# Rows of the two expert mixtures moved by list from GpSimd, with the root of a tile ahead of its two transfers

## The chip, the cores and the metric

One core of one Trainium2 chip runs the whole kernel in one launch. The metric is the device time of an execution in microseconds (us), the median of several. Lower is better.

## What is computed

Eight sequences of 512 tokens with 256 features pass through eight blocks in a row, each added to the residual stream: cross attention, a mixture of experts with layer norms inside (m0), cross attention, a "quantum" feed-forward, windowed attention, a second mixture of experts (m2), cross attention, and a ternary feed-forward. The change is in the two mixtures and in what follows them. The first one is

```python
gates = softmax(xf @ gate_w); topw, topi = top_k(gates, 2)        # 8 experts, 2 for each token
topw = topw / topw.sum(-1, keepdims=True)
h = gelu(_ln(einsum('td,edh->teh', xf, w1) + b1, ln1_g, ln1_b))   # 512 hidden features
y = einsum('teh,ehd->ted', h, w2) + b2
out = _ln(einsum('ted,te->td', y, combine) + xf, ln_g, ln_b)
```

The second has 1024 hidden features, no norm inside and none at its end. Each token is worked on by its two experts alone, so its row of 256 numbers has to come to the tiles of these experts, and the two results have to come back to the token.

## The kernel before

4096 tokens stand in SBUF as 32 tiles of 128 (`NT`), four to a batch (`TPB`), eight batches (`NB`). 8192 (token, expert) pairs fill at most 71 tiles of 128 rows (`NTILES`), each owned by one expert. A mixture has three stages, each a block with one instruction stream per engine, and the next block begins when all engines have ended this one.

1. `dispatch`. Batch by batch VectorE normalises (L909), TensorE transposes (L856) and forms the logits (L864), ScalarE copies, VectorE picks the two experts and works out the place of each pair (`route`, `ROUTE_STEPS` small operations one after the other), TensorE sums the counts (L872, L873). GpSimd then scatters the 128 rows of each tile twice into the DRAM tensor `sorted_in`, one indirect DMA for each tile and choice (L1042, 64 in all), and 8 more for padding (L1047).
2. `experts` (m0) and `experts_gelu` (m2). SyncE loads the 71 tiles in order (L1146, L1329), ScalarE stores the results to `sorted_out` (L1205, L1392). There are two buffers for tiles on their way in (`xin`) and two for results (`y`). In m0 TensorE's order at step j is: the four transposes of the hidden tile j (L1175), layer 1 of tile j+2 (L1166), the two transposes of the input tile j+3 (`turn`, L1157), layer 2 of tile j (L1185). VectorE's order at step j is: `hidden(j+2)` (bias and statistics, L1235 to L1241), the result y(j) (L1255), `centre(j+2)` (L1245). GpSimd takes the root of a tile's variance (L1271), and for the first 32 tiles it also adds a bias to two tiles of the residual stream at every second tile (L1280). At the start of the stage SyncE also loads five constants and the next attention's weights.
3. `combine_norm` (m0): GpSimd gathers two rows for each token (L1496, 64 indirect DMAs, each with its own wait for a free buffer), ScalarE scales the first (L1525), GpSimd adds it (L1507), VectorE adds the second (L1534), takes the norm (L1546, L1550), adds it to the stream (L1553) and takes the statistics of the next norm. After m2 there is no such stage: the next attention (`Arrival`) gathers the rows itself on GpSimd (L290).

TensorE's wait for tile j at `turn` is a wait for that tile's load; a load of tile j may begin when tile j-2 has been transposed (`xT_ps`, L1145). Each engine runs its own instructions strictly in the order written.

Of the kernel before, what the change touches and what calls it, by code (L numbers as in the profile page):

```python
# [23 lines left out]
P = 128  # L24
# [15 lines left out]
CAP = (NT + 1) * P  # L40
# [13 lines left out]
C_REGION = C_J + NTILES  # L54
C_PART = C_REGION + E
C_N = C_PART + 1


def constants():
# [12 lines left out]
    c[:, C_REGION:C_REGION + E] = CAP * np.arange(E)  # L72
    c[:, C_PART] = p
    return c
# [33 lines left out]
class Core:  # L108


    def __init__(self, nc, ctx, a):
# [4 lines left out]
        self.zeroed, self.padded = sem("zeroed"), sem("padded")  # L116
        self.scattered = [sem(f"scattered{s}") for s in range(2)]
        self.g_in = [sem(f"g_in{r}") for r in range(RING)]
        self.y_in = [sem(f"y_in{r}") for r in range(2 * TPB)]
        self.mixtures, self.gathers = 0, 0  # L120
# [15 lines left out]
        self.xs = nc.dram_tensor("sorted_in", [E * CAP + P, D], F32, kind="Internal").ap()  # L136
        self.ys = nc.dram_tensor("sorted_out", [NTILES * P, D], F32, kind="Internal").ap()
        self.pos = [sb(f"pos{j}", [P, NT], U32) for j in range(TOPK)]
# [12 lines left out]
RING = 4  # L151
# [45 lines left out]
def load_stage(nc, k):  # L197
# [3 lines left out]
    with ctx:  # L201
        zero_set, ones_set = sem("ld_zero_set"), sem("ld_ones")
        with nc.Block() as block:
# [12 lines left out]
            def _(pool):  # L216
# [4 lines left out]
                pool.dma_start(k.xs[E * CAP:E * CAP + P, :], k.zero[:, :]).then_inc(k.zeroed, 16)  # L221
# [52 lines left out]
class Arrival:  # L274


    def __init__(self, k, sb, sem, nm, shift):
        self.k = k
        self.got = [[sb(f"{nm}g{j}_{r}", [P, D]) for r in range(2 * TPB)] for j in range(TOPK)]
        self.scaled, self.part, self.whole = (sem(nm + c) for c in ("scaled", "part", "whole"))  # L280
        self.norm = Norm(k, sem, nm + "in", shift)

    def landed(self, eng, n):
        eng.wait_ge(self.k.y_in[n % (2 * TPB)], 32 * (n // (2 * TPB)) + 32)

    def fetch(self, pool, n):

        wait_pos(pool, self.whole, n - 2 * TPB + 1)
        for j in range(TOPK):
            pool.indirect_dma_start(  # L290
                out=self.got[j][n % (2 * TPB)][:, :], out_offset=None, in_=self.k.ys[:, :],
                in_offset=bass.IndirectOffsetOnAxis(ap=self.k.pos[j][:, n:n + 1], axis=0)
            ).then_inc(self.k.y_in[n % (2 * TPB)], 16)

    def add(self, dve, b):

        k = self.k
        for n in range(b * TPB, (b + 1) * TPB):
            self.landed(dve, n)
            for j, added in enumerate((self.part, self.whole)):  # L300
                dve.scalar_tensor_tensor(k.xt(n), self.got[j][n % (2 * TPB)][:, :], k.wt[j][:, n:n + 1], k.xt(n),
# [3 lines left out]
    def scale_first(self, act, n):  # L305

        k, got = self.k, self.got[0][n % (2 * TPB)]
# [2216 lines left out]
```

## Time and profile before

| | us |
|---|---|
| median of 3 runs | 2505.26 |
| lowest and highest | 2502.19, 2505.46 |
| the profiled execution | 2496.09 |
| its span, first to last instruction | 2494.3 |

| Engine | busy us | share of the span |
|---|---|---|
| TensorE matmul (PE) | 1960.8 | 79% |
| VectorE (DVE) | 1378.0 | 55% |
| ScalarE (ACT) | 894.4 | 36% |
| GpSimd (POOL) | 522.7 | 21% |

The busy shares are means over eight blocks with different limits, and so say little on a stage. The profile has to be cut into stages first, and the limit read in each. PEclk is TensorE's granted clock as a share of 2.4 GHz (0.50 is 1.2 GHz). The instructions that issue a DMA from SyncE or ScalarE aren't counted as busy, the indirect DMAs of GpSimd are, since their descriptors are written by that engine itself.

### The profile page before, as it was taken

The numbers are of one execution on the slowest core, as the hardware profiler recorded it, in microseconds if no ns is written. First come the engines' busy times: TensorE is split into PE (matmuls) and PEld (weight loads), VectorE is DVE, ScalarE is ACT, GpSimd is POOL, SyncE is SP. The second block draws the span as 40 slices with busy tenths as digits, with TensorE's granted clock in tenths as the row PEclk, the third lists the DMA queues.
The fourth block names the chain that finished last, engine by engine and source line by source line (L and its number), as shares of the span: only waits on it lengthen the run. The fifth ranks groups of instructions, "written<-read, shape, count | busy, mean of one in ns | idle before, by whom it ended". The sixth has DMA issues, their size and how long they took to land. (4 is left out here: it accounts for less than half of the span.)

```text
span 2494.3 us, 40430 instructions
## 1 busy us (share of the span) xinstructions
PE 1960.8 (79%) x11858; PEld 1467.3 (59%) x11859; DVE 1378.0 (55%) x3378; ACT 894.4 (36%) x1938; POOL 522.7 (21%) x560
## 2 busy tenths in 40 slices
PE   6997419999800699699979751999999994999587
PEld 4665406666500366366666441899999993565255
DVE  5875426666467477778756443222222222787787
ACT  3452104444311344333312110333333332545587
POOL 1212532211187111101100164000000004562000
PEclk9997559999955799899989655999999996999699
DMA  6000231221121400000000323111111113110001
GB/s 243 1 1 22 80 132 57 63 62 61 56 74 58 180 1 1 13 1 0 0 8 10 135 89 108 30 38 34 38 35 36 38 34 121 39 47 1 8 27 35
DMA packets 81874, 125.70 MB, mean 50 GB/s; under 512 B 17104, under 2 KB 65872, under 8 KB 78704
## 3 DMA queue, kind: packets, MB, share of 16 engines
q1 hardware_dynamic: 46640, 68.02, 8.2%
q0 software_dynamic: 13104, 35.80, 4.4%
q10 hardware_dynamic: 22032, 20.62, 2.4%
q8 instruction: 57, 0.93, 0.2%
q14 instruction: 41, 0.34, 0.0%
HBM read 82.58 MB, written 41.81 MB: 50 GB/s over the span
## 5 line engine op out<-in xcount | busy, mean ns | idle before, releaser
L1386 ACT ACTIVATE e_hT<-psum,e_bt 128x128 f32<-128x128 f32 x568 | 154.2, 383 | 335.3 <-PE psum L1349 335.3
L1349 PEld LDWEIGHTS psum<-e_xT,e_w 128*128 128x128 f32 x2272 | 267.0, 193 | 8.4 <-ACT e_xT L1379 4.9
L1349 PE MATMUL psum<-e_xT,e_w 128*128 128x128 f32 x2272 | 267.7, 276 | 4.2 <-ACT e_xT L1379 4.2
L1358 PE MATMUL psum<-m_w,e_hT 128*128 x1136 | 256.8, 379 | 0.0
L268 POOL TENSOR_TENSOR rstd<-lnt,half 128x4 f32<-128x4 f32 (+1 forms) x72 | 75.6, 1050 | 760.9 <-DVE lnt L262 760.8
L1358 PEld LDWEIGHTS psum<-m_w,e_hT 128*128 128x128 f32 x1136 | 210.4, 190 | 25.7
L1414 DVE COPY e_w<-m_w 128x2048 f32 x71 | 87.1, 1227 | 250.0 <-PE psum L1349 224.6
L698 DVE TENSOR_REDUCE a_mx<-psum 128x8 f32<-128x512 f32 x192 | 123.2, 684 | 109.4 <-PE psum L502 109.1
L483 PE MATMUL psum<-a_cx,att_wk 128*128 128x64 f32 x192 | 29.9, 305 | 165.0 <-DMA a_cx<-in_ctxT 165.0
L1212 ACT ACTIVATE e_hT<-psum,e_bt,e_gt 128x128 f32<-128x128 f32 x284 | 106.7, 456 | 140.8 <-PE psum L1175 140.8
L627 ACT ACTIVATE a_pT<-psum 128x512 f32<-128x512 f32 x192 | 104.0, 594 | 127.3 <-PE psum L552 127.2
L1185 PE MATMUL psum<-m_w,e_hT 128*128 x568 | 139.7, 389 | 4.8 <-ACT e_hT L1212 4.7
L1166 PE MATMUL psum<-m_w,e_xT 128*128 x284 | 139.7, 615 | 1.3 <-ACT e_xT L1200 1.2
L1827 PE MATMUL psum<-f_w,f_q 128*128 128x256 f32 x512 | 121.8, 383 | 14.7 <-DVE f_q L1714 14.7
L1424 DVE TENSOR_TENSOR e_y<-psum,e_b 128x256 f32<-128x256 f32 x71 | 30.2, 425 | 184.8 <-PE psum L1358 184.8
L1827 PEld LDWEIGHTS psum<-f_w,f_q 128*128 128x128 f32 x512 | 97.2, 191 | 54.8 <-issue 30.5
L483 PEld LDWEIGHTS psum<-a_cx,att_wk 128*128 128x128 f32 x192 | 26.5, 214 | 172.7 <-issue 172.7
L701 DVE TENSOR_TENSOR a_pr<-psum,a_mx 128x512 f32<-128x512 f32 x192 | 123.0, 683 | 0.7
L1814 PE MATMUL psum<-f_zT,f_w 128*128 128x512 f32 x256 | 121.9, 602 | 0.8 <-DVE f_q L1711 0.8
L420 POOL MEMSET a_va<- 128x256 f32 x6 | 1.7, 313 | 555.8 <-POOLq L226 548.9
L1185 PEld LDWEIGHTS psum<-m_w,e_hT 128*128 128x128 f32 x568 | 102.1, 189 | 21.3 <-issue 6.3
L474 PE MATMUL psum<-a_zT,att_wq 128*128 128x512 f32 x192 | 102.0, 657 | 11.2 <-ACT a_qT L604 9.1
(275 smaller groups left out, 3898.4 us busy)
## 6 DMA issues: line engine op xcount, KB each, us to landing
e_x<-sorted_in SPq DMA_DIRECT2D x142, 128.0 KB, 2.2
sorted_out<-e_y ACTq DMA_DIRECT2D x142, 128.0 KB, 1.7
m_w<-in_L_ffn_w SPq DMA_DIRECT2D x16, 1024.0 KB
m_w<-in_L_ffn_w SPq DMA_DIRECT2D x16, 512.0 KB
x_res<-in_x SPq DMA_DIRECT2D x8, 512.0 KB, 7.1
out_x<-x_res SPq DMA_DIRECT2D x8, 512.0 KB, 2.9
a_cx<-in_ctxT SPq DMA_DIRECT2D x40, 64.0 KB, 2.3
e_b<-in_L_ffn_b SPq DMA_DIRECT2D x2, 1024.0 KB, 4.2
```

What stands on the lines that cost most here:

```text
L474: mm = pe.matmul(pr_b[:, :], w["q"][:, kk, c * P:(c + 1) * P], zT[:, kk, :], start=(kk == 0), stop=(kk == DC - 1))
L627: act.activation(pT[t // 2][:, g * SLOTS:(g + 1) * SLOTS, t % 2, :], tr_b[g][:, :, :], ACT.Exp).then_inc(t_evac, 1)
L698: dve.tensor_reduce(mx[g][:, :], wide[g], AX.X, ALU.max).then_inc(s_max, 1)
L701: dve.tensor_tensor(pr[t % 2][:, g * W:(g + 1) * W].rearrange("p (h l) -> p h l", h=HPC), wide[g], mx[g][:, :, None].to_broadcast([P, HPC, ...
L1166: mm = pe.matmul(h_b[s][:, c * 512:(c + 1) * 512], xT[s][:, kk, :], w1[:, bass.ds(e * (DC * F) + (kk * F + c * 512), 512)], start=(kk == 0 ...
L1185: mm = pe.matmul(y_b[:, 0:D], hT[s][:, f, :], w2[:, bass.ds(e * (FC * D) + f * D, D)], start=(f == 0), stop=(f == FC - 1))
L1212: g = act.activation(hT[s][:, f, :], hT_b[:, f, :], ACT.Gelu, bias=bt[:, col], scale=gt[:, col] if norm else 1.0)
L1349: mm = pe.matmul(h_b[s][:, f, :], w1[:, kk, f * P:(f + 1) * P], xT[s][:, kk, :], start=(kk == 0), stop=(kk == DC - 1))
L1358: mm = pe.matmul(y_b[s][:, 0:D], hT[s][:, f, :], k.w2[:, bass.ds(e * (FC * D) + f * D, D)], start=(f == 0), stop=(f == FC - 1))
L1386: g = act.activation(hT[s][:, f, :], h_b[s][:, f, :], ACT.Gelu, bias=bt[:, bass.ds(e * FC + f, 1)])
L1814: mm = pe.matmul(hb[f % HS][:, :], w1[:, kk, f * P:(f + 1) * P], zT[s][:, kk, :], start=(kk == 0), stop=(kk == DC - 1))
L1827: mm = pe.matmul(yb[t % 2][:, 0:D], q[s][:, g, t * P:(t + 1) * P], w2[:, g, :], start=(g == 0), stop=(g == FC - 1))
```

## The change

The rows are no longer sorted in DRAM. `dispatch` stores the normalised tokens as they are (direct stores by SyncE, one for each batch, tensor `rows_in`), and makes two lists for each of the 71 tiles: the token of each row (`src`) and the place of its result (`dst`). ScalarE now does the normalisation, the selection of experts runs once for each half of the tokens instead of once for each batch, and the lists come from comparisons with index constants and small bf16 matmuls in eight chunks. The 72 scatters are gone. The experts' constants are loaded here, after the first batch has been stored and after the weights (`k.late`).

In the expert stages SyncE's loads and ScalarE's stores are gone. GpSimd gathers the rows of each tile by `src` (`fetch_rows`) and scatters the results by `dst` (`send_rows`). In `experts_gelu` its order at step j is the gather of tile j+3, then the scatter of tile j. In `experts`, at step j, it is the root of tile j+2, the scatter of tile j-1, the gather of tile j+3, and the bias.

`combine_norm` and `Arrival` read the results, which now stand in the tokens' order, by direct loads of four tiles on SyncE (`expert_rows`). In `combine_norm` the normalisation goes to ScalarE, the product with the gain to GpSimd, each over whole batches, with three buffers. Behind them the 64 gathers of each are gone.

The core of the diff (in `dispatch` and `Arrival` cut to a few lines):

```diff
@@ dispatch
-                            pool.indirect_dma_start(
-                                out=k.xs[:, :], out_offset=bass.IndirectOffsetOnAxis(ap=sent_to[j][:, n:n + 1], axis=0),
-                                in_=zk[b % len(zk)][:, t * D:(t + 1) * D], in_offset=None).then_inc(k.scattered[b % 2], 16)
+                for b in range(NB):
+                    sp.wait_ge(z_done, b + 1)
+                    sp.dma_start(k.zs[P + b * SEQ:P + (b + 1) * SEQ, :].rearrange("(t p) d -> p t d", p=P),
+                                 z[b % Z].rearrange("p (t d) -> p t d", t=TPB)).then_inc(stored[b % 2], 16)
+                    if b == 0:
+                        k.late(sp)
+                        load_expert_constants(sp, k, L)
...
+                    dve.tensor_tensor(at_tile[s][:, :, :], k.cst[:, None, C_J:C_J + NTILES].to_broadcast([P, NJ, NTILES]),
+                                      tile_of[:, own, None].to_broadcast([P, NJ, NTILES]), ALU.is_equal).then_inc(hot_done, 1)
+                    dve.tensor_tensor(at_slot[s][:, :, :], k.cst[:, None, C_I:C_I + P].to_broadcast([P, NJ, P]),
+                                      slot[:, own, None].to_broadcast([P, NJ, P]), ALU.is_equal).then_inc(slot_done, 1)
@@ experts
-                    with pool.Fori(0, NT // 2) as i:
-                        root(i * 2, 0)
-                        root(i * 2 + 1, 1)
-                        xs = k.x[:, bass.ds(i * (2 * D), 2 * D)].rearrange("p (t d) -> p t d", t=2)
-                        pool.tensor_tensor(xs, xs, post_b[:, None, :].to_broadcast([P, 2, D]), ALU.add)
...
+                for j in range(A + 1):
+                    fetch_rows(pool, k, j, xin, xT_ps)
+                pool.wait_ge(k.const_in, k.consts)
+                for j in range(A):
+                    root(j)
+                for j in range(NTILES):
+                    if j + A < NTILES:
+                        root(j + A)
+                    if j > 0:
+                        send_rows(pool, k, j - 1, y, y_done)
+                    if j + A + 1 < NTILES:
+                        fetch_rows(pool, k, j + A + 1, xin, xT_ps)
+                    if j % 2 and j // 2 < NT // 2:
+                        bias(j // 2)
+                send_rows(pool, k, NTILES - 1, y, y_done)
+                rows_sent(pool, k)
+def fetch_rows(pool, k, j, xin, taken):
+    wait_pos(pool, taken, j - 1)
+    pool.indirect_dma_start(
+        out=xin[j % 2][:, :], out_offset=None, in_=k.zs[:, :],
+        in_offset=bass.IndirectOffsetOnAxis(ap=k.src[:, j:j + 1], axis=0)).then_inc(k.row_in[j % 2], 16)
+def send_rows(pool, k, j, y, ready):
+    pool.wait_ge(ready, j + 1)
+    pool.indirect_dma_start(
+        out=k.ys[:, :], out_offset=bass.IndirectOffsetOnAxis(ap=k.dst[:, j:j + 1], axis=0),
+        in_=y[j % 2][:, :], in_offset=None).then_inc(k.row_out[j % 2], 16)
@@ experts_gelu
+                for j in range(3):
+                    fetch_rows(pool, k, j, xin, xT_ps)
+                for j in range(NTILES):
+                    if j + 3 < NTILES:
+                        fetch_rows(pool, k, j + 3, xin, xT_ps)
+                    send_rows(pool, k, j, y, y_done)
@@ combine_norm
+                    for j in range(TOPK):
+                        sp.dma_start(got[j][b % R][:, :, :], expert_rows(k, j, b)).then_inc(y_in[b % R], 16)
```

In `experts`, `A` is 2 in m0 (`norm`).

## Rows read from the trace of the kernel before

**Rows 1.** Header of the page, the whole execution.

```profile
span 2494.3 us, 40430 instructions
```

**Rows 2.** Busy time by stage: from:to, length, busy (instructions), PEclk, DMA share, GB/s.

```profile
217.53:350.53 133.00, 52.28 (x226) 47.84 (x226) 57.77 (x261) 15.97 (x17) 70.10 (x72) 0.50 0.20 71
350.53:681.87 331.34, 305.63 (x1278) 206.04 (x1278) 192.97 (x426) 135.11 (x356) 58.73 (x87) 0.96 0.22 70
681.87:825.14 143.27, 0.00 (x0) 0.00 (x0) 91.57 (x256) 16.25 (x32) 104.24 (x112) 0.50 0.20 60
...
1412.30:1546.00 133.70, 52.31 (x226) 47.85 (x226) 57.46 (x261) 16.64 (x17) 70.39 (x72) 0.50 0.36 134
1546.00:2080.90 534.90, 517.70 (x3550) 487.42 (x3550) 117.29 (x142) 174.96 (x640) 0.00 (x0) 0.98 0.13 39
2080.90:2320.90 240.00, 187.32 (x1472) 121.19 (x1472) 165.87 (x427) 100.83 (x193) 116.42 (x125) 0.89 0.16 51
```

**Rows 3.** Timeline of one tile of `experts` (m0): start, length, engine, line.

```profile
396.42 1.95 PE L1166 MATMUL psum<-m_w,e_xT 128*128 x4
...
398.20 0.38 PE L1157 MATMUL psum<-cst,e_x 128*128 128x128 f32 x2
...
398.42 1.95 PE L1185 MATMUL psum<-m_w,e_hT 128*128 x8
...
400.46 0.55 POOL L1271 TENSOR_TENSOR e_rs<-e_ve,half 128x1 f32<-128x1 f32 x1 [2.52 <-DVE e_ve L1241]
...
400.64 1.88 PE L1166 MATMUL psum<-m_w,e_xT 128*128 x4
```

**Rows 4.** Instruction groups of GpSimd, by shape: busy, mean ns, idle before.

```profile
L1280 POOL TENSOR_TENSOR x_res<-x_res,e_post_b 128x512 f32 x16 | 20.3, 1269 | 0.0
```

**Rows 5.** Timeline of `combine_norm`: a second gather and the first reader of both.

```profile
683.97 0.96 POOL L1496 DMA_INDIRECT c_g<-sorted_out,pos  x1 [0.31 <-issue]
...
686.81 0.51 ACT L1525 ACTIVATE c_g<-c_g,wt 128x256 f32<-128x256 f32 x1 [9.80 <-DMA c_g<-sorted_out,pos]
```

**Rows 6.** TensorE by stretch: length, busy (instructions), PEclk, DMA share, GB/s.

```profile
679.10:681.20 2.10, 0.04 (x1) 1.00 0.18 62
681.20:690.00 8.80, 0.00 (x0) 0.50 0.32 89
...
368.70:377.40 8.70, 8.10 (x12) 0.50 0.10 30
377.40:381.40 4.00, 2.87 (x12) 1.00 0.14 33
1555.70:1561.80 6.10, 5.54 (x25) 0.50 0.07 21
```

**Rows 7.** Timeline, layer 1 of a tile of m0 at the start of the stage.

```profile
373.50 3.77 PE L1166 MATMUL psum<-m_w,e_xT 128*128 x4 [0.56 <-ACT e_xT L1200]
```

**Rows 8.** Instruction groups of the first `dispatch`.

```profile
L864 PE MATMUL psum<-r_gate,r_zT 128*128 128x8 f32 x128 | 28.7, 362 | 9.2 <-ACT r_zT L893 9.2
...
L856 PE MATMUL psum<-cst,r_z 128*128 128x128 f32 x64 | 15.7, 427 | 31.4 <-DVE r_z L909 22.4 <-DMA r_gate<-in_L_gate 5.3 <-issue 3.7
...
L1023 DVE TENSOR_TENSOR r_moved<-r_hot,r_shift 128x256 f32<-128x256 f32 x2 | 0.8, 425 | 0.2
```

**Rows 9.** Timeline, end of the first `dispatch`: last scatter, first DMA of the next stage.

```profile
341.69 0.96 POOL L1047 DMA_INDIRECT sorted_in<-zero,r_pad  x1 [0.30 <-issue]
350.53 0.33 SPq L1134 DMA_DIRECT2D e_b<-in_L_ffn_b  x1
```

**Rows 10.** DMA view of the second `dispatch`: GB/s in 40 slices of 3.4 us.

```profile
GB/s 126 427 427 427 427 422 347 117 80 120 118 78 0 39 112 83 78 39 115 79 78 78 117 96 78 101 117 39 45 110 117 78 92 102 109 85 117 78 0 7
```

**Rows 11.** Instruction groups of VectorE in `combine_norm`.

```profile
L1546 DVE TENSOR_SCALAR x_z<-x_z,mean,rstd (+1 forms) x32 | 11.4, 419 | 0.7
...
L1550 DVE TENSOR_TENSOR x_z<-x_z,c_g 128x1024 f32 (+1 forms) x8 | 9.9, 1233 | 1.1 <-DVE x_z L1546 0.2
```

**Rows 12.** Timeline of the attention after m2: GpSimd's first root.

```profile
2101.96 1.04 POOL L268 TENSOR_TENSOR rstd<-lnt,half 128x4 f32<-128x4 f32 x1
```

More of the change, by code:

```diff
@@ L879, in _ @@
-                pe.wait_ge(w_in, 16)
-                for b in range(2):
-                    turn(b, b)
-                    logits(b, b)
-                over_batches_ahead(pe, step)
-                pe.wait_ge(v, ROUTE_STEPS * NB + 1)
-                pe.matmul(pp[0][:, 0:E], k.cst[:, C_ONE:C_ONE + P], cnt[3][:, :],
-                          start=True, stop=True).then_inc(cnt_ps, 1)
+                flat = lambda t: t[:, :, :].rearrange("p t e -> p (t e)")
+                turn(0, 0)
+                pe.wait_ge(w_in, 16)
@@ new lines, in _ @@
+                for b in range(NB):
+                    if b + 1 < NB:
+                        turn(b + 1, (b + 1) % 2)
+                    logits(b, b % 2)
+                pe.wait_ge(chosen_done, 1)
+                pe.matmul(pp[:, 0:NT * E], k.cst[:, C_TRI:C_TRI + P], flat(chosen), start=True, stop=False)
+                pe.wait_ge(chosen_done, 2)
+                pe.matmul(pp[:, 0:NT * E], k.cst[:, C_ONE:C_ONE + P], flat(total), start=False, stop=True)
+                pe.matmul(pp[:, NT * E:NT * E + E], k.cst[:, C_ONE:C_ONE + P], ahead[STEPS % 2][:, NT - 1, :],
+                          start=True, stop=True).then_inc(place_ps, 1)
@@ new lines, in _ @@
+                dve.wait_ge(place_ps, 1)
+                for s in range(2):
+                    dve.wait_ge(stored[s], 16 * NB // 2)
+                both = lambda t: t[:, :, :, :].rearrange("p j t e -> p j (t e)")
+                each = lambda t: t[:, :, :, :].rearrange("p j t e -> p (j t) e")
+                tiles = cnt[0]
+                then(dve.tensor_copy(tiles[:, :], pp[:, NT * E:NT * E + E]))
+                then(dve.tensor_tensor(both(prod), both(hot), pp[:, None, 0:NT * E].to_broadcast([P, TOPK, NT * E]), ALU.mult))
@@ L1059, in over_tiles @@
+                then(dve.tensor_tensor(k.dst[:, :], row[:, :], over[:, :], ALU.add))
+CHUNKS, STEPS = 8, 5
 def over_tiles(eng, step, ahead):
@@ L1288, in experts_gelu, with rows_sent @@
+def rows_sent(pool, k):
+    for s in range(2):
+        pool.wait_ge(k.row_out[s], 16 * (k.mixtures + 1) * ((NTILES + 1 - s) // 2))
 def experts_gelu(nc, k):
```

668 lines of the change are left out of this document (295 added, 373 removed).

## The prediction

> **What bounds the kernel now.** I read the header for the span [rows 1], cut the span into stages by SyncE's first DMA of each, and asked for the busy time of every engine in each stage [rows 2]. Three things are to be seen. The two `dispatch` stages (133.0 and 133.7 us) run no engine above 53% busy, GpSimd with its 72 indirect DMAs (70 us) is the busiest. `combine_norm` (143.3 us) is bound by GpSimd (104.2 us busy) and VectorE (91.6 us), which take turns. The expert stages are bound by TensorE: 305.6 of 331.3 us in m0, 517.7 of 534.9 us in m2. Then I read one tile of m0 in the timeline [rows 3]: layer 1 of one tile starts at 396.42 and of the next at 400.64, a period of 4.2 us in which TensorE never rests, while input tiles were loaded long before they were needed. The chain of waits ends in the last stage, which the change doesn't touch, so every stage counts with its own length.
>
> **The experts of m0: the new order closes a ring.** Take what GpSimd now does at step j: root(j+2), scatter(j-1), gather(j+3). The root waits for the variance of tile j+2, so for `hidden(j+2)` on VectorE, so for layer 1 of tile j+2 on TensorE. The gather of tile j+3 is queued behind that root. TensorE's next instruction after layer 1 of tile j+2 is `turn(j+3)`, which waits for this very gather. Nothing was prefetched: the buffer had been free since `turn(j+1)`, a whole step before, but GpSimd stood in the root's wait. Behind `turn(j+3)` stand layer 2 of tile j, the hidden transposes of tile j+1 and layer 1 of tile j+3, whose end releases the next root. This is one ring per tile, and its length is a sum:
>
> - Layer 1 ends at 396.42 + 1.95 = 398.37, the root at 400.46 + 0.55 = 401.01 [rows 3]: 2.64 us, spent on VectorE's bias, statistics and variance and on the root.
> - The scatter and the gather each take 0.96 us of GpSimd with 0.30 us between two [rows 5, 9]: 0.16 + 0.96 + 0.30 = 1.42 us from the root's end to the gather's start (the 0.16 is my estimate for the first gap, below the 0.30 of the row).
> - From the start of a gather to its first reader: 686.81 - 683.97 = 2.84 us [rows 5]. There the queue ahead held another gather. Here it holds a scatter; I take the same, and bound it by one more 0.96 us.
> - From `turn` to the end of the next layer 1 at full clock: 398.20 to 400.64 + 1.88 = 402.52, 4.32 us [rows 3].
>
> The sum is 11.22 us at full clock, and TensorE idles in 6.9 us of it. Now the clock. It fell 2.1 us after the last matmul of this stage [rows 6], so an idle stretch of 6.9 us should lose it each time. It came back 8.7 us after TensorE started again at 368.7 and 6.1 us after 1555.7 [rows 6]. The first of these was itself broken by waits. At half clock layer 1 takes 3.77 instead of 1.95 us [rows 3, 7], so the 4.32 us become 8.6. If the clock returns t us into a burst, t/2 is lost: nothing lost gives 11.2 us, all at half clock gives 15.5. A burst here is dense from its start, so I take a return after 5 us, a little less than the better of the two rows, and get 11.2 + 2.5 = 13.7 us.
>
> The Trainium skill (TensorE: Matmul & The Clock Gate, HAM oscillation — how this bites in real kernels) describes just such a loop, whose wait for a DMA sends the clock down in every iteration, so that each burst starts slow. By that rule the period lies above 11.2 us, without it it is 11.2 us. The rows of the fall agree with it.
>
> 68 tiles (gathers 3 to 70) go through the ring. Beside them stand the start (first gather, then three layers 1 of 3.8 us at half clock with the transposes between: about 19 us), the last two tiles (12 us) and the end. At the end there is something new: after GpSimd's last indirect DMA of `dispatch` (341.69 + 0.96 = 342.65) the next stage began only at 350.53, 7.9 us later [rows 9]. The expert stage now ends with a scatter and pays that, in all about 9 us. Sum: 68 x 13.7 + 40 = 972 us against 331.3, so +640. The root, the bias (1.27 us at every second of the first 32 tiles [rows 4], 20 us in all if the 6.9 us of waiting didn't hide it) and ScalarE's gelus are beside the ring. The earlier constants save some 12 us of start-up, which the 19 already contain.
>
> **What gets shorter.**
>
> - First `dispatch`: no scatters. TensorE becomes the bound of its first part: logits 28.7 and transposes 15.7 us at half clock [rows 8], 44 us and 5 us for the first batch. Then a serial tail on VectorE. A 256-element operation takes 0.43 us [rows 8], a 1024-element one 1.23 us [rows 11], in between I interpolate. Second selection 4, scan 4, matmul 2, ranks and tile numbers 7, eight chunks of 0.75 + 1.23 = 16 us, which I stretch to 21 for GpSimd's product beside them, lists and end 4 us. Together 91 us, between 80 (chunks unstretched, steps overlapping) and 110 (chunks doubled). The 7.9 us at the end go too [rows 9]. 133 - 91 = 42 us gained.
> - Second `dispatch`: SyncE's queue now holds store 0, the weights, the constants, store 1. The weights take 20 us at 427 GB/s [rows 10], and normalising batch 3 waits for store 1, its buffer: about 9 us more than the first, 100 us. 134 - 100 = 34 us gained.
> - `combine_norm`: VectorE keeps its 91.6 us [rows 2] less the 11.4 and 9.9 us that go elsewhere [rows 11], so 70 us, with some 24 us for the first loads and sums, the last batch and small waits: 94 us, between 85 and 110. GpSimd's whole-batch operations stay below that. 49 us gained.
> - Attention after m2: the first root was at 2101.96, 21 us into the stage [rows 12], behind 16 gathers of 1.26 us. Two direct loads and the same sums bring it to about 7 us; with the end's drain that goes as well I take 19 us of the 240 [rows 2], between 8 and 30.
> - `experts_gelu`: here the gather of tile j+3 stands ahead of the scatter of tile j and no root is in the way. From y(j-2) to `turn(j+2)` lie two layers 1 and one layer 2, so some 1.5 tiles of 517.7 / 71 = 7.3 us [rows 2], 11 us, against 5 us for the sum, the scatter, the gather and its landing: hidden. Start -5, end +6, none of 534.9 us gained.
>
> Gained together: 42 + 34 + 49 + 19 = 144 us. Against the profiled execution's own time: 2496.1 + 640 - 144 = 2992 us. The median of the runs shown lies 9.2 us above it, so 3001 us.
>
> **The rivals.**
>
> 1. *The clock holds through the ring* (it needs that 6.9 us of rest don't lower it, against the 2.1 us of rows 6). Period 11.2 us, 68 x 11.2 + 35 = 797 us, +465; 2496 + 465 - 144 + 9 = 2826 us.
> 2. *The clock never comes back within a burst.* The 8.7 us of rows 6 speak for it, a burst at half clock being 8.6 us long. Period 15.5 us, 1096 us, +765; 3126 us.
> 3. *The gathers are hidden, and the kernel gets faster.* Place: GpSimd in the experts of m0. It needs 0.55 + 0.16 + 0.96 + 0.30 + 0.96 us and half of a bias [rows 3 to 5], 3.6 us a tile, within the 4.2 us. If the gather of tile j+3 started more than 2.84 us before the end of layer 1 of tile j+2, nothing would wait; from that point on the stage would be 331 - 12 + 6 = 325 us and the kernel 2496 - 144 - 6 + 9 = 2355 us. What speaks against it is the order written: the gather can't start before the root, nor the root before that layer 1 has ended. It decides only if I have misread which tile's root stands there.
> 4. *The gains in the other stages don't come*, as VectorE and GpSimd slow each other where both now work on whole batches, and the lists take longer than the scatters did. With none of the 144 us gained, 3145 us at my period.
>
> For the third the Trainium skill (DMA: Bandwidth & Descriptors, Issuing engines are not separate DMA queues) has a rule: all DMAs run on the same 16 engines, and which engine issues one changes only the issuer's time, "usually small relative to the DMA itself". By that rule alone moving the loads from SyncE to GpSimd would cost next to nothing and the kernel would come out at the third rival's time. In these rows a queue isn't only its issue time: what counts is what the issuer waits for first.
>
> **How the numbers follow.** My forecast, return of the clock somewhere inside the burst: 0.60, with a range of its own of 2930 to 3080 us (returns between 3 and 7 us are 68 us either way, the other bounds some 30). Rival 1: 0.14. Rival 2: 0.15. Rival 3: 0.06. Rival 4: 0.05. The range 2820 to 3130 us takes in rivals 1 and 2. A difference under 0.2% (5 us) can't be told from no change. Only rival 3 is faster: 0.06; no case lies within 0.2%, I leave 0.01; slower 0.93.
>
> **What would show it right or wrong.** In the changed kernel's timeline of m0's experts: layer 1 every 13 to 14 us; `turn` released by the DMA of its tile, not by an engine, with 6 to 7 us of idle before it, 68 times; the gather starting 1.4 us after the root; a granted clock between 0.5 and 1.0 for the stage, changing in each tile. In m2 the period stays 7.3 us and the stage within a few us of 535. The `dispatch` stages are near 91 and 100 us, `combine_norm` near 94 us. I am wrong in the mechanism if `turn` doesn't wait for its gather, and in size if the landing after a scatter is much longer than 2.84 us or the clock behaves as in rivals 1 and 2.

## The result, and the profile after

The changed kernel takes 2989.6 us (median of four runs, 2984.2 to 2992.4) against 2504.1 us on the same chip (2502.2 to 2505.5). The ratio is 1.194, with a 95% interval of 1.1915 to 1.1958. Predicted were 3001 us.

The header of the page, which answers to [rows 1]:

```profile
span 2990.6 us, 37832 instructions
```

The busy time by stage answers to [rows 2]. The columns are from:to, length, then busy time (instructions) of PE, PEld, DVE, ACT and POOL, PEclk, DMA share and GB/s. In order: first `dispatch`, `experts` of m0, `combine_norm`, the attention, quantum and windowed blocks together, second `dispatch`, `experts_gelu`, the attention after m2.

```profile
216.50:300.47 83.97, 52.31 (x262) 48.57 (x262) 41.55 (x86) 30.25 (x49) 16.42 (x8) 0.50 0.26 90
300.47:1269.22 968.75, 451.72 (x1278) 281.26 (x1278) 184.85 (x426) 135.49 (x356) 202.92 (x229) 0.74 0.07 21
1269.22:1365.07 95.85, 0.00 (x0) 0.00 (x0) 82.27 (x216) 29.68 (x64) 62.45 (x40) 0.50 0.29 89
1365.07:1955.13 590.06, 527.58 (x2800) 351.11 (x2800) 392.97 (x934) 206.42 (x365) 63.34 (x45) 0.93 0.06 23
1955.13:2059.45 104.32, 49.63 (x262) 45.74 (x262) 41.53 (x86) 30.26 (x49) 16.42 (x8) 0.52 0.35 132
2059.45:2595.50 536.05, 519.01 (x3550) 488.73 (x3550) 117.28 (x142) 175.46 (x640) 140.61 (x142) 0.98 0.12 37
2595.50:2817.00 221.50, 187.28 (x1472) 121.17 (x1472) 165.22 (x426) 100.84 (x193) 54.10 (x61) 0.92 0.17 56
```

One stage grew, the experts of m0, from 331.3 to 968.8 us. TensorE has the same 1278 instructions in it, but is busy for only 451.7 us of it, at a mean granted clock of 0.74. The two `dispatch` stages, `combine_norm` and the attention after m2 are shorter by 144.3 us together, `experts_gelu` is 1.2 us longer, and the three blocks between are 2.9 us longer.

Where the time went is one group of TensorE's instructions in this stage, `turn` (busy and mean ns, then the idle time before it and what ended it):

```profile
L1136 PE MATMUL psum<-cst,e_x 128*128 128x128 f32 x142 | 48.7, 447 | 487.8 <-DMA e_x<-rows_in,src 487.8
```

TensorE stood still for 487.8 us in front of `turn`, always until the DMA of a gather. One tile in the timeline answers to [rows 3]:

```profile
699.31 1.88 PE L1145 MATMUL psum<-m_w,e_xT 128*128 x4
...
703.29 0.56 POOL L1242 TENSOR_TENSOR e_rs<-e_ve,half 128x1 f32<-128x1 f32 x1 [9.61 <-DVE e_ve L1213]
704.04 1.04 POOL L1277 DMA_INDIRECT rows_out<-e_y,dst  x1 [0.20 <-issue]
705.39 0.97 POOL L1269 DMA_INDIRECT e_x<-rows_in,src  x1 [0.30 <-issue]
708.23 0.69 PE L1136 MATMUL psum<-cst,e_x 128*128 128x128 f32 x2 [7.04 <-DMA e_x<-rows_in,src]
...
709.24 3.33 PE L1164 MATMUL psum<-m_w,e_hT 128*128 x8 [0.32 <-issue]
...
712.84 1.88 PE L1145 MATMUL psum<-m_w,e_xT 128*128 x4
```

Layer 1 (L1145) ends at 701.19. GpSimd's root (L1242) waits for it by way of VectorE, the scatter and the gather stand behind the root, and `turn` (L1136) waits for the gather. The next layer 1 starts 13.53 us after the last. TensorE by stretch in the same tile, the columns as above:

```profile
701.20:705.10 3.90, 0.00 (x0) 0.00 (x0) 1.72 (x4) 0.00 (x0) 1.60 (x2) 1.00 0.01 2
705.10:708.20 3.10, 0.00 (x0) 0.00 (x0) 0.00 (x0) 0.00 (x0) 0.97 (x1) 0.51 0.27 85
708.20:712.00 3.80, 3.45 (x9) 2.52 (x10) 0.00 (x0) 0.38 (x1) 0.00 (x0) 0.50 0.00 0
712.00:714.70 2.70, 2.70 (x11) 1.31 (x9) 0.88 (x2) 1.51 (x4) 0.00 (x0) 1.00 0.00 0
```

The granted clock falls 3.9 us after layer 1 has ended, to 0.50 (1.2 GHz), and is back at 1.00 (2.4 GHz) 3.8 us into the burst. So `turn` and most of layer 2 run at half speed, and layer 1 at full speed. It is so in nearly every tile; in three of the last ones of the stage the half clock lasts longer (10.2 us), and layer 1 falls into it too. A period counted over gathers is 13.68 us (tiles 5 to 31) and 13.72 us (tiles 36 to 68).

### The profile page after: what moved, and what is told of

The parts are those of the page before. It is cut to its first block and busy times, and to the rows that moved or that the text cites. A ratio compares the mean times of both kernels' runs of the same rounds, so it can differ in the third digit from the quotient of the medians.

```text
span 2990.6 us, 37832 instructions
## 1 busy us (share of the span) xinstructions
PE 2102.6 (70%) x11915; PEld 1541.1 (52%) x11931; DVE 1326.8 (44%) x2988; ACT 936.8 (31%) x2034; POOL 595.4 (20%) x580
## 5 line engine op out<-in xcount | busy, mean ns | idle before, releaser
L1136 PE MATMUL psum<-cst,e_x 128*128 128x128 f32 x142 | 48.7, 447 | 487.8 <-DMA e_x<-rows_in,src 487.8
L1227 DVE TENSOR_TENSOR e_y<-psum,x_b 128x256 f32<-128x256 f32 x71 | 30.1, 425 | 671.6 <-PE psum L1164 670.9
L1136 PEld LDWEIGHTS psum<-cst,e_x 128*128 128x128 f32 x142 | 20.8, 204 | 546.6 <-DMA e_x<-rows_in,src 536.1
L1164 PE MATMUL psum<-m_w,e_hT 128*128 x568 | 243.9, 604 | 24.1 <-issue 20.5
L1373 ACT ACTIVATE e_hT<-psum,x_bt 128x128 f32<-128x128 f32 x568 | 154.6, 383 | 336.4 <-PE psum L1336 322.5
L1345 PE MATMUL psum<-m_w,e_hT 128*128 x1136 | 256.8, 379 | 0.0
L1345 PEld LDWEIGHTS psum<-m_w,e_hT 128*128 128x128 f32 x1136 | 210.4, 190 | 25.7
L1164 PEld LDWEIGHTS psum<-m_w,e_hT 128*128 128x128 f32 x568 | 174.9, 323 | 89.1 <-issue 51.9
L1179 ACT ACTIVATE e_xT<-psum 128x256 f32<-128x256 f32 x71 | 27.3, 384 | 552.6 <-PE psum L1136 552.6
L1187 ACT ACTIVATE e_hT<-psum,x_bt,x_gt 128x128 f32<-128x128 f32 x284 | 106.9, 457 | 276.7 <-PE psum L1154 276.7
L1242 POOL TENSOR_TENSOR e_rs<-e_ve,half 128x1 f32<-128x1 f32 x71 | 39.8, 561 | 717.6 <-DVE e_ve L1213 717.6
L1269 POOL DMA_INDIRECT e_x<-rows_in,src x142 | 139.4, 982 | 62.7 <-issue 41.9
L1277 POOL DMA_INDIRECT rows_out<-e_y,dst x106 | 108.2, 1021 | 193.4 <-DVE e_y L1404 175.0
L1145 PE MATMUL psum<-m_w,e_xT 128*128 x284 | 138.6, 611 | 1.3 <-ACT e_xT L1179 1.2
## 6 DMA issues: line engine op xcount, KB each, us to landing
m_w<-in_L_ffn_w SPq DMA_DIRECT2D x16, 1024.0 KB, 15.3
```

What stands on the lines that cost most here:

```text
L1145: mm = pe.matmul(h_b[s][:, c * 512:(c + 1) * 512], xT[s][:, kk, :], w1[:, bass.ds(e * (DC * F) + (kk * F + c * 512), 512)], start=(kk == 0 ...
L1164: mm = pe.matmul(y_b[:, 0:D], hT[s][:, f, :], w2[:, bass.ds(e * (FC * D) + f * D, D)], start=(f == 0), stop=(f == FC - 1))
L1187: g = act.activation(hT[s][:, f, :], hT_b[:, f, :], ACT.Gelu, bias=bt[:, col], scale=gt[:, col] if norm else 1.0)
L1269: pool.indirect_dma_start(out=xin[j % 2][:, :], out_offset=None, in_=k.zs[:, :], in_offset=bass.IndirectOffsetOnAxis(ap=k.src[:, j:j + 1], ...
L1277: pool.indirect_dma_start(out=k.ys[:, :], out_offset=bass.IndirectOffsetOnAxis(ap=k.dst[:, j:j + 1], axis=0), in_=y[j % 2][:, :], in_offse ...
L1345: mm = pe.matmul(y_b[s][:, 0:D], hT[s][:, f, :], k.w2[:, bass.ds(e * (FC * D) + f * D, D)], start=(f == 0), stop=(f == FC - 1))
```

## The experiments

The theory: a ring of root, scatter, gather, `turn`, layer 2 and layer 1 sets the period, and the clock's return adds to it. The rivals for the cause: the clock alone, the number of input buffers, or simply that GpSimd now moves the rows. Unless said otherwise an edit is in `experts` of m0 alone, and starts from the changed kernel. The stage lengths below are that stage's.

**The change unchanged, on the chip of three others.**

> The changed kernel as it is, beside the others, since the kernel before took 2478 us with the first four runs and 2504 us at first: 2990 us again, with m0's experts at 969 us, if the change's own stages don't differ between two chips; up to 1% less if whatever made the kernel before faster there acts on both.

2989.4 us, ratio 1.1965 (1.193 to 1.200), stage 967.2 us. The kernel before took 2498.0 us there, and 2478.2 us on the chip of the next three experiments and of the one with 13 added matmuls. Differences of 1% are therefore read by stage, or on one chip.

**The gather first, the rest as it was.**

```diff
+                    if j + A + 1 < NTILES:
+                        fetch_rows(pool, k, j + A + 1, xin, xT_ps)
                     if j + A < NTILES:
                         root(j + A)
                     if j > 0:
                         send_rows(pool, k, j - 1, y, y_done)
-                    if j + A + 1 < NTILES:
-                        fetch_rows(pool, k, j + A + 1, xin, xT_ps)
```

> In the experts of m0 GpSimd's order at step j becomes gather(j+3), root(j+2), scatter(j-1); all else is as in the changed kernel. Theory of the ring (turn of a tile waits for a gather that stands behind a root): the gather of tile j+3 now stands behind the root of tile j+1 and the scatter behind that, so the ring spans two tiles: 2.64 us to the root's end, 1.4 us to the gather, 2.84 us to its landing, 4.32 us to the end of layer 1, 11.2 us for two tiles, 5.6 us a tile, and 0.6 us a tile more for the first 32 tiles, where the bias stands in between. Stage 68 x 5.6 + 20 + 35 = 436 us against 969, kernel 2457 us. Rival, the price is what GpSimd's transfers cost as such (issue and landing, whatever the order): the period stays near 13.7 us and the kernel near 2990 us. Rival, any order with the gather ahead of its own step's root hides it wholly: 4.2 us a tile, kernel about 2346 us.

2552.0 us (ratio 1.030, 1.027 to 1.032), stage 535.1 us.

**Gather, scatter, root.**

```diff
-                    if j + A < NTILES:
-                        root(j + A)
-                    if j > 0:
-                        send_rows(pool, k, j - 1, y, y_done)
                     if j + A + 1 < NTILES:
                         fetch_rows(pool, k, j + A + 1, xin, xT_ps)
+                    if j > 0:
+                        send_rows(pool, k, j - 1, y, y_done)
+                    if j + A < NTILES:
+                        root(j + A)
```

> In the experts of m0 GpSimd's order at step j becomes gather(j+3), scatter(j-1), root(j+2). Theory of the ring: the gather of tile j+3 stands right behind the root of tile j+1: 2.64 + 0.2 + 2.84 + 4.32 = 10.0 us for two tiles, 5.0 us a tile, 0.6 us more for the first 32 tiles. Stage 68 x 5.0 + 20 + 35 = 395 us, kernel 2416 us. The same rivals as for the first: 2990 us if the order doesn't matter, 2346 us if one gather ahead of one root is enough.

2484.3 us (ratio 1.003, 1.002 to 1.004), stage 466.5 us. The order of three instructions is worth 434 us of the stage in the first of these kernels and 502 us in this one. In both the time was above what I expected, by 95 and 68 us, and the mean granted clock of the stage is 0.84 and 0.90. The timeline of this last kernel shows why:

```profile
414.42 0.44 PE L1136 MATMUL psum<-cst,e_x 128*128 128x128 f32 x2 [2.69 <-DMA e_x<-rows_in,src]
...
415.43 3.55 PE L1164 MATMUL psum<-m_w,e_hT 128*128 x8 [0.56 <-issue]
...
419.25 1.88 PE L1145 MATMUL psum<-m_w,e_xT 128*128 x4
...
420.97 0.38 PE L1136 MATMUL psum<-cst,e_x 128*128 128x128 f32 x2
```

One tile waits 2.69 us, the next (420.97) doesn't wait at all. After the wait layer 2 takes 3.55 us instead of 1.99, so the clock fell for it. Long tiles of 9.4 us and short ones of 4.2 us (layer 1 to layer 1) take turns up to tile 36; behind it, without the bias, two tiles mostly take 10.9 to 12.7 us and the clock falls less often. I had spread the wait evenly over all tiles and left the clock out.

**The gather a tile earlier still.** The input buffer of tile j+4 is free when `turn(j+2)` is done, which TensorE does in its step j-1. So the gather of tile j+4 goes first, with the same two buffers.

```diff
                 for j in range(A):
                     root(j)
+                fetch_rows(pool, k, A + 1, xin, xT_ps)
                 for j in range(NTILES):
-                    if j + A < NTILES:
-                        root(j + A)
+                    if j + A + 2 < NTILES:
+                        fetch_rows(pool, k, j + A + 2, xin, xT_ps)
                     if j > 0:
                         send_rows(pool, k, j - 1, y, y_done)
-                    if j + A + 1 < NTILES:
-                        fetch_rows(pool, k, j + A + 1, xin, xT_ps)
+                    if j + A < NTILES:
+                        root(j + A)
```

> In the experts of m0 GpSimd's order at step j becomes gather(j+4), scatter(j-1), root(j+2), with the gather of tile 3 ahead of the first step; still two buffers for input tiles. The gather of tile j+4 now begins about 2.8 us after the end of layer 1 of tile j+1 and lands 5.7 us after it, while its turn comes only 8.4 us after it. Theory of the ring: nothing waits for a gather any more, TensorE is the bound again with 4.2 us a tile (4.3 with GpSimd 3.9 us busy of it), stage 320 to 335 us against 969, kernel 2346 us (2335 to 2370), so 6% faster than the kernel before, since the 140 us that the other stages gained remain. Rival: GpSimd with 2.5 us of transfers, the root and the bias in a tile becomes the bound itself, 5 us a tile, kernel about 2400 us.

2345.5 us, ratio 0.946 (0.943 to 0.949): it beats both kernels. Its stage, with the columns of the stages above, and two `turn`s of its timeline:

```profile
298.98:624.22 325.24, 304.69 (x1278) 204.80 (x1278) 193.23 (x426) 135.50 (x356) 203.14 (x229) 0.98 0.20 61
```

```profile
404.11 0.38 PE L1136 MATMUL psum<-cst,e_x 128*128 128x128 f32 x2
404.12 1.01 POOL L1270 DMA_INDIRECT e_x<-rows_in,src  x1 [0.17 <-issue]
...
408.33 0.38 PE L1136 MATMUL psum<-cst,e_x 128*128 128x128 f32 x2
```

No idle time stands before `turn`, the period is 4.2 us, and the granted clock stays at 1.00 once the stage is running. GpSimd does the same 203 us of work as in the changed kernel. So neither the move to GpSimd nor the number of buffers costs the 640 us, only the place of the gather in GpSimd's queue.

**Three input buffers, root still first.** After the root and the scatter comes the gather of tile j+4 into a third buffer (`xin[j % 3]`, its own three semaphores, TensorE's loop unrolled by six).

```diff
-        xin = [sb(f"{nm}x{s}", [P, D]) for s in range(2)]
+        xin = [sb(f"{nm}x{s}", [P, D]) for s in range(3)]
...
-                    if j + A + 1 < NTILES:
-                        fetch_rows(pool, k, j + A + 1, xin, xT_ps)
+                    if j + A + 2 < NTILES:
+                        fetch(j + A + 2)
```

> The changed kernel's order (root, scatter, gather) with three buffers for input tiles, so that the gather at step j is that of tile j+4. The ring of 11.4 us then spans two tiles. Theory of the ring: 5.7 us a tile bare; the first variant, whose bare ring over two tiles was as long, took 7.0 us a tile where no bias stood in it, its clock falling once in two tiles, so I expect 6.9 us here for all tiles (the bias is behind the gather): stage 505 us, kernel about 2525 us, and 2440 us if the clock holds. Rival (depth is no remedy, since GpSimd's transfers themselves are slow or the root is late whatever is prefetched): 13.7 us a tile, kernel 2990 us.

2512.8 us (ratio 1.006, 1.004 to 1.008), stage 496.4 us, against the 505 us expected. The gather still stands behind the root, but the ring now goes once round in two tiles. They alternate between 9.4 and 4.2 us, as with gather, scatter, root up to tile 36, where the bias (1.27 us at every second tile) stood in the place of the scatter.

**Root, gather, scatter.** The gather is one scatter (1.34 us) nearer to the root.

```diff
                     if j + A < NTILES:
                         root(j + A)
-                    if j > 0:
-                        send_rows(pool, k, j - 1, y, y_done)
                     if j + A + 1 < NTILES:
                         fetch_rows(pool, k, j + A + 1, xin, xT_ps)
+                    if j > 0:
+                        send_rows(pool, k, j - 1, y, y_done)
```

> In the experts of m0 GpSimd's order at step j becomes root(j+2), gather(j+3), scatter(j-1): of the changed kernel's ring only the scatter, 1.35 us with its gap, is taken out. Theory: the bare ring goes from 11.4 to 10.0 us, the idle stretch from 6.9 to 5.6 us, in which the clock still falls (it fell in the first variant, where TensorE idles 4 us at a time); with 2.4 us lost to it as before the period is 12.4 us, stage 880 us, kernel 2900 us. Rival: the clock's return sets the period and not the ring (13.65 us in the changed kernel, the same to 0.1 us from tile to tile), and shortening the ring gives nothing: 13.7 us, kernel 2990 us. Second rival, the loss to the clock grows by less than the ring shrinks and stays half clock for longer: above 13.7 us.

2982.5 us (ratio 1.194, 1.190 to 1.197), stage 962.6 us, period 13.66 us. I expected 2900 us, and the rival held. One tile in its timeline:

```profile
703.60 0.69 PE L1136 MATMUL psum<-cst,e_x 128*128 128x128 f32 x2 [5.69 <-DMA e_x<-rows_in,src]
...
704.61 3.77 PE L1164 MATMUL psum<-m_w,e_hT 128*128 x8 [0.33 <-issue]
...
709.03 2.34 PE L1145 MATMUL psum<-m_w,e_xT 128*128 x4
```

The wait is 1.35 us shorter than in the changed kernel, as worked out. But layer 2 takes 3.77 us instead of 3.33 and layer 1 2.34 instead of 1.88: all that the wait lost, the burst pays back at the lower clock. The stage's mean granted clock is 0.65 instead of 0.74.

**TensorE kept busy.** Matmuls whose result nobody reads stand ahead of `turn`. The kernel computes them besides what is wanted. Nothing else moves. If the clock costs something, more work on TensorE makes the kernel faster.

```diff
+        unread = ps(nm + "unread", [P, 512])
...
                     if more(A + 1):
+                        for i in range(13):
+                            pe.matmul(unread[:, :], k.ident, w1[:, 0:512], start=True, stop=True)
                         turn(j + A + 1, (s + A + 1) % 2)
```

> The changed kernel with GpSimd's order as it is, and 13 more matmuls of 128x512 on TensorE in each tile of m0's experts, between layer 1 of tile j+2 and the transposes of tile j+3, whose result nobody reads. At full clock they fill 6.4 of the 6.9 us in which TensorE waits for its gather. Theory (2.5 us of the 13.7 us period are lost to the clock, which falls in every wait): the clock stays full, the ring takes its bare 11.2 us, stage 68 x 11.2 + 35 = 797 us against 969, kernel 2818 us, faster although TensorE does 66% more work in the stage. Rival (the clock plays no part, the ring is 13.7 us of waits): the added work is hidden at best, period 13.7 us, kernel 2990 us, or more if it isn't hidden.

3093.4 us (ratio 1.248). Here my edit was mis-sized: each of these matmuls is two instructions of 0.44 us in the trace, so 13 of them take 11.4 us and are longer than the wait they were to fill. It shows only that at a granted clock of 0.99 a period of 15.3 us is possible. With 7:

> As the run with 13 added matmuls a tile (period 15.3 us, clock full throughout), with 7 of them: there each 32-bit matmul showed as two instructions of 0.44 us, so the 13 took 11.4 us instead of the 6.4 us meant, and the ring was theirs. 7 take 6.2 us, inside the 6.9 us in which TensorE waits for its gather. Theory (some 2.4 us of the 13.7 us period are lost to the clock, which falls in every wait): the clock stays full and the period is the bare ring, 2.7 to the root's end, 1.5 to the gather, 2.84 to its landing, 4.3 to the end of layer 1, 11.4 us; stage 68 x 11.4 + 35 = 810 us against 969, kernel about 2830 us, although TensorE does about twice the matmul work in the stage. Rival (the clock plays no part in the period): 13.7 us a tile, kernel 2990 us.

2889.0 us (ratio 1.156, 1.153 to 1.160), stage 869.4 us at a granted clock of 0.98. 6.17 us of useless work in each tile make the kernel 100 us faster than the changed one on the same chip. Its timeline gives the bare ring:

```profile
700.82 1.88 PE L1146 MATMUL psum<-m_w,e_xT 128*128 x4
...
702.54 6.17 PE L1161 MATMUL psum<-m_w,cst 128*128 128x512 f32 x14
...
709.73 0.44 PE L1137 MATMUL psum<-cst,e_x 128*128 128x128 f32 x2 [1.02 <-DMA e_x<-rows_in,src]
...
710.69 1.99 PE L1167 MATMUL psum<-m_w,e_hT 128*128 x8 [0.52 <-issue]
...
712.95 1.88 PE L1146 MATMUL psum<-m_w,e_xT 128*128 x4
```

From the end of layer 1 (700.82 + 1.88 = 702.70) to `turn` it is 7.03 us, as in the changed kernel. From `turn` to the end of the next layer 1 (714.83) it is 5.10 us. The bare ring is 12.13 us, where I had summed 11.22. The term that was wrong is the last one: layer 2 starts 0.96 us after `turn`, and 0.22 us after it in [rows 3].

**Only three such matmuls** (2.64 us of the 7.0).

```diff
-                        for i in range(7):
+                        for i in range(3):
```

> The changed kernel's order, with 3 matmuls of 128x512 f32 ahead of turn whose result nobody reads (computed besides what is wanted). 3 of these are six instructions of 0.44 us, 2.64 us. With 7 the granted clock stayed at 1.0 and the period was 12.1 us, the bare ring; with none it alternates in every tile and the period is 13.65 us. Of the 6.9 us that TensorE waits, 4.3 us are left idle. Theory: what counts is the length of the idle stretch; 4.3 us is enough to lower the clock, since 2.1 us were enough after the stage before; then the fall comes later and the return is as late, the period stays between 13.2 and 13.7 us and the kernel at 2950 to 2990 us. Rival: the loss follows how much of the period TensorE is busy; with 2.6 us more it is, and the clock falls in one tile of two as in the orders with the gather first, period 12.8 us, kernel about 2930 us, or not at all, 12.1 us and 2880 us.

2990.8 us (ratio 1.197, 1.193 to 1.200), stage 972.8 us, period 13.68 us (tiles 5 to 31). The mean granted clock is higher than in the changed kernel, 0.85 instead of 0.74, and it buys nothing, since the half clock still falls on the burst. Layer 2 takes 3.42 us.

**The owner's number read ahead of `turn`.** Between `turn` and layer 2 TensorE reads from SBUF which expert owns tile j. In [rows 3] that is invisible. This starts from the kernel with 7 unread matmuls, whose clock stays full.

```diff
+                    e = pe.value_load(k.owner[0:1, bass.ds(j, 1)], min_val=0, max_val=E - 1)
                     if more(A + 1):
                         for i in range(7):
                             pe.matmul(unread[:, :], k.ident, w1[:, 0:512], start=True, stop=True)
                         turn(j + A + 1, (s + A + 1) % 2)
-                    e = pe.value_load(k.owner[0:1, bass.ds(j, 1)], min_val=0, max_val=E - 1)
```

> The kernel with 7 unread matmuls ahead of turn (computed besides what is wanted, results unread), in which the granted clock stays full and the bare ring is 12.13 us a tile; the number of the expert that owns tile j, which TensorE's layer 2 reads from SBUF into a register, is now read before these matmuls and turn, not behind turn. In every kernel where turn waits, layer 2 starts 0.96 to 1.04 us after turn's start instead of the 0.22 us of the kernel before. Theory: the register read (and the addresses worked out from it) is done ahead of time where TensorE's sequencer isn't held by a wait, and stands in the ring where turn waits; read ahead, layer 2 starts 0.3 to 0.5 us after turn, the ring is some 11.5 us, the kernel 68 x 0.6 = 40 us under the 2889 us, 2850 us. Rival: the late start belongs to the transposes' own pipeline or to another wait; nothing moves, 2889 us.

2828.2 us (ratio 1.132, 1.130 to 1.134), stage 811.4 us, and the period is 11.39 us in both halves of the stage. The timeline:

```profile
708.81 0.44 PE L1137 MATMUL psum<-cst,e_x 128*128 128x128 f32 x2 [1.03 <-DMA e_x<-rows_in,src]
709.08 1.93 PE L1167 MATMUL psum<-m_w,e_hT 128*128 x8
...
711.28 1.88 PE L1146 MATMUL psum<-m_w,e_xT 128*128 x4
```

Layer 2 now starts 0.27 us after `turn`, and the next layer 1 ends 4.35 us after it. This is the 4.32 us of my sum. One line, moved ahead of a wait, saves 61 us against 2889.0 (40 expected), 58 of them in this stage.

**The other order in m2.** This starts from the kernel of 2345.5 us; the edit is in `experts_gelu`.

```diff
-                    if j + 3 < NTILES:
-                        fetch_rows(pool, k, j + 3, xin, xT_ps)
                     send_rows(pool, k, j, y, y_done)
+                    if j + 3 < NTILES:
+                        fetch_rows(pool, k, j + 3, xin, xT_ps)
```

> The kernel with the gather of tile j+4 first (2345.5 us), and in the experts with 1024 hidden features the scatter of tile j now stands ahead of the gather of tile j+3. The same ring is meant to close there with another wait in its place. Theory: the scatter waits for y(j), so for the end of layer 2 of tile j; from there 0.66 us to y, 1.3 us for the scatter's issue and the gap, 2.84 us from the gather's start to its reader, 4.9 us in all. If TensorE wants the gather of j+3 one layer after layer 2 of j (some 3.6 us of the 7.3 us a tile), it idles 1.3 to 1.5 us a tile, the period is about 8.8 us, the stage 640 us and the kernel 2450 us. Rival: TensorE's order there wants tile j+3 only a whole tile later, everything is hidden, the stage stays at 536 us and the kernel at 2345 us. This tells whether 'a transfer that TensorE needs next stands behind an engine's result' is enough, or whether the slack has to be counted.

2557.9 us (ratio 1.024, 1.021 to 1.027), 212 us more than without the edit, where 105 were expected. The stage is 750.5 us long (1414.04 to 2164.55) against 536.3. The first line is a stretch of this length that begins and ends 4 us earlier, the others are from one tile:

```profile
1410.40:2160.70 750.30, 588.72 (x3558) 518.73 (x3558) 120.16 (x151) 175.81 (x640) 140.57 (x142) 0.94 0.08 27
```

```profile
1802.13 0.99 POOL L1278 DMA_INDIRECT rows_out<-e_y,dst  x1 [7.50 <-DVE e_y L1405]
1803.42 0.97 POOL L1270 DMA_INDIRECT e_x<-rows_in,src  x1 [0.30 <-issue]
...
1806.26 0.44 PE L1328 MATMUL psum<-cst,e_x 128*128 128x128 f32 x2 [1.51 <-DMA e_x<-rows_in,src]
...
1807.30 3.72 PE L1346 MATMUL psum<-m_w,e_hT 128*128 x16 [0.61 <-ACT e_hT L1374]
```

The wait of 1.51 us is the one that I worked out (1.3 to 1.5). Behind it come again a late start of layer 2 (1.04 us after `turn`) and, in some tiles, a lower clock. Most periods are 9.6 to 9.8 us, some 11.4, the mean 10.4 against 7.25. In the change a gather of this stage starts at 2304.74 and its `turn` at 2313.14, 5.6 us after the 2.84 us of its landing. The reverse order uses this slack up, since the gather then stands behind the result of its own step, one tile (7.25 us) later than the result of the step before.

**The kernel before, once more.**

> The kernel before, unchanged, so that its stages can be laid beside those of the other kernels on the same chip. It has come out at 2504, 2498 and 2478 us on different chips. Theory: the difference lies in the stages whose clock falls and comes back (start-ups and the last stage), not in the experts of m0, which stay at 331 us within 1 us.

2495.3 us, ratio 0.999 (0.998 to 1.001). The experts of m0 take 331 us here as well. The 1% between chips isn't explained: this run fell on a chip where the kernel before takes 2498 us, and none was profiled on the one with 2478 us.

## Why the prediction was right, point by point

- *The ring*: right. Every `turn` from tile 3 on waits for its gather's DMA, 68 times. The idle time before it is 7.04 us (6.9 predicted), the gather's start lies 1.54 us after the root's end (1.42), and from there to the reader it is 2.84 us, exactly the value of [rows 5], with a scatter ahead instead of a gather. Moving the gather ahead of the root takes 434 or 502 us off the stage, and a tile earlier removes the wait.
- *The period*: 13.7 predicted, 13.7 measured, but two of its terms were off and cancelled, and the way they are added is not borne out. The bare ring is 12.1 us, not 11.2. The term "from `turn` to the end of the next layer 1" was read in a kernel in which `turn` never waited. There TensorE's read of the owner's number was done ahead of time. Behind a wait it costs 0.7 us in each tile, as the kernel with the early read shows. The clock costs the other way less: it came back after 3.8 us of the burst, not 5, and the burst is 1.4 us longer than at full clock (6.49 against 5.10), not 2.5. It fell 3.9 us after the last matmul here, not 2.1 as in [rows 6], which changes nothing in the sum. With the measured terms the sum is 13.5 us, but the period isn't a bare ring plus a loss: a ring shorter by 1.35 us left it where it was, only with the clock held is it the ring's own length. That the sum gave 13.7 us is luck.
- The Trainium skill (TensorE: Matmul & The Clock Gate, HAM oscillation — how this bites in real kernels) counts half of the time at the lower clock as lost. Half of 3.8 us is 1.9, the runs show 1.4. Its "every single K-tile" holds for the changed kernel. In the orders with the gather first the loss came in one tile of two, as the wait did.
- *The stage*: 972 predicted, 968.8 measured, of which 68 x 13.7 = 932 were to be the ring. The start took 18 us (19 predicted), the 68 tiles 934, the last two 11 (12). For the end I had charged 9 us and it took 6. From the end of the last scatter (1263.70 + 0.97 = 1264.67) to the first DMA of the next stage (1269.22) it is 4.6 us, against the 7.9 us read off [rows 9] for `dispatch`.
- *First `dispatch`*: 91 predicted, 84.0 measured. The eight chunks took 22 us, as predicted (21). Shorter than summed were the serial steps between the last logits and the first chunk, 15 us (259.8 to 274.7) against 17, and the part before them. *Second `dispatch`*: 100 predicted, 104.3 measured.
- *`combine_norm`*: 94 predicted, 95.9 measured, though VectorE is busy for 82 us instead of the 70 that I gave it. The difference is in its smallest operations, here as instruction groups (busy, mean ns, idle before) of this stage of the changed kernel,

```profile
L256 DVE TENSOR_TENSOR mean<-stats 128x4 f32<-128x4 f32 x16 | 15.4, 963 | 0.0
L254 DVE TENSOR_TENSOR lnt<-stats 128x4 f32<-128x4 f32 x16 | 13.5, 844 | 0.6
```

and in the timeline (start, length, engine, line):

```profile
1299.88 2.35 POOL L1478 TENSOR_TENSOR x_z<-x_z,c_g 128x1024 f32<-128x1024 f32 x1
1300.25 2.00 DVE L254 TENSOR_TENSOR lnt<-stats 128x4 f32<-128x4 f32 x1
1302.19 2.35 POOL L1482 TENSOR_TENSOR x_z<-x_z,c_g 128x1024 f32<-128x1024 f32 x1
1302.26 2.31 DVE L256 TENSOR_TENSOR mean<-stats 128x4 f32<-128x4 f32 x1
```

  Both operations on four columns end together with GpSimd's product over a whole batch, at 1302.2 and 1304.6, and take 0.15 to 0.17 us where GpSimd is idle. In the two groups that makes 24 us, against which the second add is 8 us shorter (15.5 instead of 23.7 us). So part of the fourth rival was there. The stage is hardly longer for it, as VectorE was not busy for 13.6 us of it, where the prediction had allowed 24. The Trainium skill (SBUF — State Buffer, SBUF: two separate sides) says that VectorE, in an operation with two inputs in SBUF, and GpSimd, in one that reads SBUF, share a pair of ports as an exclusive lock for the whole instruction. These rows agree.
- *Attention after m2*: 221 predicted, 221.5 measured, though the first root came at 12.2 us of the stage, not at 7, so 9 us earlier and not 14. The second batch's normalisation starts 12.8 us earlier (21.3 us into the stage against 34.1), and where the rest of the 18.5 us comes from wasn't followed up. *`experts_gelu`*: 0 predicted, +1.2 us measured, hidden as argued. The reverse order shows that a whole tile's later start is more than this slack.
- *The rivals*: the first (clock holds, 2826 us) and the second (never back, 3126 us) are out by the rows of one tile. The first one's time is what came out when the clock was held and the owner's number read early, 2828 us. The third's condition (the gather starts over 2.84 us before the end of layer 1 of tile j+2) isn't met in the change; the kernel that meets it takes 2345.5 us, where the third rival had 2355. The fourth is out as a whole: 144 us of gains were predicted, 144.3 came. That they agree so closely is luck: the four stages gained 49.0, 29.4, 47.4 and 18.5 us where 42, 34, 49 and 19 were predicted.

Open is why the period of the changed order stays at 13.7 us. Three kernels with bare rings of 12.1, 10.8 (worked out for the gather before the scatter) and 12.1 us (three unread matmuls) all have it, with quite different shares of the time at half clock. What these share is seen when the granted clock is read stretch by stretch. The columns are from:to, length, PE busy (instructions), PEclk, DMA share and GB/s. The four pairs of lines are of the changed kernel, of root, gather, scatter, of the three unread matmuls, and of gather, scatter, root:

```profile
698.32:705.15 6.83, 2.87 (x12) 1.00 0.00 1
705.15:711.98 6.83, 3.43 (x9) 0.50 0.12 38
...
767.97:778.21 10.24, 6.37 (x16) 0.50 0.08 26
778.21:781.62 3.41, 1.25 (x3) 1.00 0.00 0
...
698.06:708.30 10.24, 5.86 (x19) 1.00 0.08 26
708.30:711.72 3.42, 2.93 (x7) 0.50 0.00 0
...
401.55:404.96 3.41, 3.19 (x8) 0.50 0.14 38
404.96:415.20 10.24, 7.21 (x30) 1.00 0.11 38
```

In all four it is 13.65 us from one fall of the granted clock to the next, however it divides into half and full clock. In the first three kernels this is one tile, in the fourth it is two, the long one and the short one, and with three input buffers it is two as well (412.14 to 425.79). So the length that doesn't move is that of the clock's fall and return, and the tiles keep step with it: what one gains in the wait, the burst loses again. What sets this length and ties the tiles to it, the runs don't show.

## What to carry to other kernels

When a prefetch is moved to an engine that also computes, write down for each transfer what its issuer waits for just before it, and follow that wait back: if it ends in the instruction that needs this transfer, nothing is prefetched, and a third buffer only spreads the loss over two tiles. The transfer whose buffer has been free longest goes first, which bought 644 us here, while a wait that was merely shortened (from 7.0 to 5.7 us) bought nothing, since the clock still fell for it. A duration read where an engine never waits leaves out what its sequencer did ahead of time, so register reads are counted behind a wait, or moved in front of it.

## What the runs showed of the hardware that I had not expected

- 6.17 us of matmuls that nobody reads, in each of 68 tiles, made the kernel 100 us faster (2889.0 against 2989.4 us), and 2.64 us of them nothing (2990.8).
- The period stayed at 13.66 to 13.7 us when the wait was 1.35 us shorter: layer 2 went from 3.33 to 3.77 us and layer 1 from 1.88 to 2.34 us.
- A register read on TensorE costs 0.7 us a tile behind a wait (period 12.13 us with it there, 11.39 us with it ahead of the wait), and isn't seen where `turn` doesn't wait (layer 2 starts 0.22 us after `turn` in [rows 3]).
- From one fall of the granted clock to the next it was 13.65 us in kernels that waited 7.04, 5.69 and 2.69 us at a time.
- A VectorE operation on 4 columns with two inputs in SBUF took 2.0 to 2.3 us instead of 0.17 beside a GpSimd product of 2.35 us.
- The unchanged kernel before came out at 2504, 2498 and 2478 us on different chips, while the changed one took 2989 us on two of them.
